# Two mixture-of-experts layers: more expert pairs ahead of the edge loop, exponentials at earlier places in it, and another order of the last combining

## The reference

```python
h = (x @ W_gat).reshape(M, 4, 4)                      # M rows, 4 heads, 4 experts
e = leaky_relu(a_src[src] + a_dst[dst])               # for each edge, and each token's own loop
alpha = softmax of e over the edges that share dst
agg = segment_sum(h[src] * alpha, dst)
scores = layernorm(agg + b_gat).mean over heads       # one number for each token and expert
w = softmax(top-2 of scores)                          # the gates
for ei in range(4):
    hh = gelu(x @ W1[ei] + b1[ei])                    # 256 -> 512
    out = out + gate[ei] * (hh @ W2[ei] + b2[ei])     # 512 -> 256
```

## Time and profile before

| | us |
|---|---|
| median of three runs | 4740.75 |
| profiled execution | 4737.15 |
| its span | 4735.4 |
| PE busy | 3592.8 (76%) |
| DVE busy | 3010.6 (64%) |
| ACT busy | 1489.1 (31%) |
| POOL busy | 1360.7 (29%) |

### The profile page before, as it was taken

How to read it: one execution, slowest core, us unless ns; L and a number is a source line. 1 busy time by engine, 2 the same in 40 slices (tenths; PEclk the granted TensorE clock), 3 DMA queues, 4 the chain that set the end, 5 groups by cost and what they waited for, 6 DMA issues and landing times. The chain is left out here.

```text
span 4735.4 us, 52627 instructions
## 1 busy us (share of the span) xinstructions
PE 3592.8 (76%) x17914; PEld 2038.7 (43%) x17914; DVE 3010.6 (64%) x6268; ACT 1489.1 (31%) x2073; POOL 1360.7 (29%) x1016
## 2 busy tenths in 40 slices
PE   5999999999589678862294984859868766157796
PEld 2333333333266346541162653646535544135464
DVE  3666666676588887889020277768988888602127
ACT  2556555555253012220041321225202121012221
POOL 2766667677300000007404101000000003723210
PEclk9999999999699888875697996869998887578898
DMA  3000000000351000001111183244100001111147
GB/s 126 10 28 28 19 10 28 27 28 19 114 179 53 8 19 32 31 28 13 19 63 28 62 326 131 76 173 143 42 5 36 23 27 26 13 25 57 36 156 281
DMA packets 144861, 301.63 MB, mean 64 GB/s; under 512 B 20580, under 2 KB 103140, under 8 KB 139492
## 3 DMA queue, kind: packets, MB, share of 16 engines
q1 hardware_dynamic: 98212, 180.78, 10.7%
q10 hardware_dynamic: 25920, 94.38, 5.2%
q0 software_dynamic: 20480, 23.14, 2.5%
HBM read 183.42 MB, written 114.81 MB: 63 GB/s over the span
## 5 line engine op out<-in xcount | busy, mean ns | idle before, releaser
L1083 PE MATMUL l_pu<-l_tt,l_w 128*128 128x512 f32 x2048 | 1034.2, 631 | 366.6 <-issue 187.8
L1094 PE MATMUL l_pd<-l_w,l_hid 128*128 128x256 f32 x4096 | 985.6, 385 | 164.8 <-ACT l_hid L1273 117.9
L1094 PEld LDWEIGHTS l_pd<-l_w,l_hid 128*128 128x128 f32 x4096 | 795.5, 194 | 501.3 <-issue 415.7
L1273 ACT ACTIVATE l_hid<-l_pu,l_b 128x512 f32<-128x512 f32 x512 | 349.7, 686 | 1661.6 <-PE l_pu L1083 1268.6
L389 DVE TENSOR_TENSOR at_pr<-at_ps,at_decay 128x1024 f32<-128x1024 f32 x512 | 601.1, 1217 | 182.2 <-PE at_ps L503 181.3
L1029 POOL DMA_INDIRECT l_g<-hs_rows,l_i_src x336 | 317.5, 945 | 1344.7 <-DVEq L1732 1236.7
L1083 PEld LDWEIGHTS l_pu<-l_tt,l_w 128*128 128x128 f32 x2048 | 407.1, 203 | 678.4 <-issue 655.9
L307 ACT ACTIVATE at_ab<-at_pr 128x1024 f32<-128x1024 f32 x512 | 537.2, 1055 | 439.7 <-DVE at_pr L389 392.5
L258 POOL TENSOR_TENSOR at_ab<-at_ab 128x1024 f32<-128x1024 f32 x256 | 600.8, 2370 | 178.2 <-ACT at_ab L307 178.2
L503 PE MATMUL at_ps<-at_qr,at_kr 32*128 32x512 f32 x2048 | 349.4, 644 | 14.8 <-issue 9.8
L1870 DVE SCALAR_TENSOR_TENSOR l_xo<-l_yb,l_gates,l_xo 128x256 f32<-128x256 f32 x448 | 187.3, 481 | 154.3 <-DMA l_yb<-ys 147.1
(11 more groups left out here) (341 smaller groups left out, 4191.1 us busy)
## 6 DMA issues: line engine op xcount, KB each, us to landing
ys<-l_yst ACTq DMA_DIRECT2D x112, 512.0 KB
l_yb<-ys SPq DMA_DIRECT2D x28, 2048.0 KB, 10.2
l_tt<-tT ACTq DMA_DIRECT2D x36, 512.0 KB, 3.3
at_xt<-in_x SPq DMA_DIRECT2D x16, 1024.0 KB, 5.4
l_xt<-x SPq DMA_DIRECT2D x32, 512.0 KB, 4.1
tT<-l_xnT ACTq DMA_DIRECT2D x32, 512.0 KB, 4.4
l_xo<-x SPq DMA_DIRECT2D x28, 512.0 KB, 4.6
x<-at_xt SPq DMA_DIRECT2D x8, 1024.0 KB, 4.3
```

The costliest lines, as they stand in the source:

```text
L1083: ins = pe.matmul(ps_u[q % 2][:, :], w1[:, e, c, P * q:P * q + P], tt[:, s, c, :], start=(c == 0), stop=(c == KK - 1))
L1094: ins = pe.matmul(out, hid[:, k % 2, c, P * r:P * r + P], w2[:, k % GE, c, :], start=False, stop=(c == MB - 1), skip_group_check=True)
L1273: act.activation(hid[:, k % 2, q, :], ps_u[q % 2][:, :], ACT.Gelu, bias=b1[:, k % GE, q:q + 1]).then_inc(s_act, 1)
```

## The change

The number of pairs ahead of the loop goes from 32 to 40, that in the loop from 24 to 16; direct pairs stay 8. The step counts follow: two more steps in the node blocks, 13 instead of 6 single steps in the first list, 14 instead of 10 in the late stage; what is left after the histogram goes from 14 steps to 33 (4 x 40 + 4 = 164 steps in all, of which 131 stand earlier). The exponentials stand after 24 and 40 of the loop's 68 steps, before after 41 and 66 of 100. The output buffers go from three to two. SP waits before its first loads of the tail only for the stores made ahead of the loop, and for the others before block 10. DVE and POOL take the ten stored blocks of the first pairs first, and the other four between the direct pairs. New lines shift the numbers after the change by 2 to 5.

```diff
-PRE_PAIRS = PAIRS // 2
+PRE_PAIRS = PAIRS // 2 + 8
-YB = 3
-PRE_NODES = (0, 0, 0, 1, 1, 1, 1, 1, 2, 2, 2, 2, 2, 2, 2, 2)
+YB = 2
+PRE_NODES = (0, 0, 0, 1, 1, 1, 2, 2, 2, 2, 2, 2, 2, 2, 2, 2)
-PRE_LATE = 10
+PRE_LATE = 14
-IN_SCAN = 41
-IN_MERGE = 66
+IN_SCAN = 24
+IN_MERGE = 40
...
-        TAIL_ORDER = [d for i in range(DIRECT) for d in [("stored", t) for t in range(i * STORED // DIRECT, (i + 1) * STORED // DIRECT)] + [("direct", i)]]
+        REST = STORED - BP
+        TAIL_ORDER = [("stored", t) for t in range(BP)] + [
+            d for i in range(DIRECT) for d in [("stored", BP + t) for t in range(i * REST // DIRECT, (i + 1) * REST // DIRECT)] + [("direct", i)]]
...
             for k in range(YB):
-                sp.wait_ge(s_y[k], n * (16 * LOOPED // YB) + 16 * ((PRE_PAIRS + YB - 1 - k) // YB))
-                sp.sem_inc(s_turn, 1)
+                sp.wait_ge(s_y[k], 16 * ((PRE_PAIRS + YB - 1 - k) // YB))
...
             for t in range(STORED):
                 b = t % 3
+                if t == BP:
+                    for k in range(YB):
+                        sp.wait_ge(s_y[k], n * (16 * LOOPED // YB) + 16 * ((PRE_PAIRS + YB - 1 - k) // YB))
+                        sp.sem_inc(s_turn, 1)
...
-                if h % (2 * IDX // RANK) == 2 * IDX // RANK - 1:
+                if h % (IDX // RANK) == IDX // RANK - 1:
                     pre(1)
...
-            pre(UNITS0 // 2)
+            pre(UNITS0)
```

## The result

The changed kernel takes 4703.18 us (median of 4 runs, 4700.86 to 4705.43), the kernel before on the same chip 4739.18 (4 runs, 4737.59 to 4741.27). The ratio is 0.9924, 95% interval 0.9907 to 0.9941: 36 us less, where 40 were forecast. The profiled execution took 4702.14, its span 4699.5.

The account below looks back on a forecast made before the run. The bound changes place: PE hangs on late ACT during gathers; DVE waits for exponentials and stored results. Per layer +85 - 86 - 20 = -21, for two -42: 4737.15 to 4695, median 3.6 above, 4699; range 4652 to 4744.

Parts of the forecast that it names:

- Ahead of the loop, +85: Work before the loop: 32 added steps per layer delay the start of POOL's gathers by 85 us.
- The last steps: After the histogram, 33 steps instead of 14: 19 uncovered steps at 3.44 us, +65.4 us per layer.
- The late steps: Late stage, 4 more steps: 13.8 us, inside PE's 18.27 us wait for DVE, so cost 0.
- nodes and list: Node blocks' two second steps, +2.7 us; first list's 7 more single steps at 2.4 us, +16.9 (bounds 0 and 29).
- In the loop, -86: Loop, per layer: earlier exponentials save 56 us at the first and 31 at the second, less 1 for the odd step.
- The odd shift of 17 steps: In the loop: ACT's late answer may fall on a step pair's other half, shifting the second exponential some 11 us either way.
- Gates, -1: When the gates are ready: +85 - 86 = -1 us, nearly where they were, at about 4521 in the old count.
- Tail, -20: Gates to end of span: 88 us for ten stored blocks plus 106 after, 194 against 213.8, so -20 per layer.
- The forecast of the ring: Tail buffers: combining 7.1, store 7.6, load 11.5, a round of 26.2 us; ten stored blocks take 88 us.
- Fast ring: Rival, 18%: tail loads keep up with DVE, ten blocks take 69 us instead of 88, 38 us less in all, 4661.
- Nothing left: Rival, 15%: single steps cost 29 us instead of 17, ten blocks 96 instead of 88; +20 a layer, 4737.
- Direct pairs at their old spacing: Rival, 12%: in the tail eight direct pairs take 138 us instead of 94; net +46 in all, 4787.

Follow-up runs that it names:

- new tail alone: Kernel before plus only SP's early loads and the new combining order, three buffers kept: 4692.8 us (0.9906) with late ACT, 4370.5 us (0.9895) with ACT in pace.

## Why the prediction was right, step by step

- **Ahead of the loop, +85.** Measured from the layer's start to the first gather: 923.2 - 840.4 = +82.8 in the first layer, +89.6 in the second. The last steps: +64.9 for 65.4. The late steps: covered. The rest, nodes and list, came to 18 and 25 us for 19.6; of it DVE's waits in the first list are 32.9 - 17.6 = 15.3 and 34.2 - 14.9 = 19.3, for 16.9.
- **In the loop, -86.** Measured 461.9 - 548.4 = -86.5 in the first layer and -86.0 in the second. The two waits are 55.2 and 22.1, where 57 and 20 were forecast. The odd shift of 17 steps did not move ACT's late answers by a noticeable amount.
- **Gates, -1.** Counted from each layer's own start (1276.3 and 3117.8, before 1275.9 and 3137.9) they moved by -3.7 us in the first layer and +3.6 in the second. The new tail alone, with none of the first two parts, has its gates at 4500.4, and the changed kernel on that same chip has them at 4500.9. This is the direct proof that the two large terms cancel there.
- **Tail, -20.** Ten blocks 87 us for 88, PE stood 26.45 for 26, gates to end 4699.5 - 4504.67 = 194.8 for 194; before 214.2, so -19.4. In the first layer, from its gates to the start of the second, 473.2 went to 456.4: -16.8. So the layers gained 20.5 and 15.8 us where 21 each were forecast, and most of the 6 us missing is in the +89.6 and the -16.8. The forecast of the ring, a round of 26.2 us for three buffers, held against the rival in which the ring keeps up with DVE (69 us). DMA engines were at 0.93 there: the loads are what DVE waited for. Some luck is in these hits. The first buffer's three rounds took 20.9, 33.5 and 25.8 us, 26.7 in the mean. A load took 13.1 us and a store 5.1 in the median, where 11.5 and 7.6 were put in, and only their sum was right. After the ten blocks the prediction's terms (2.3, 89.5, 4, 1.0 and 8.1) add up to 105 and not to the 106 it wrote; 107.2 were measured, and the single stored blocks, taken at 4 us, cost PE nothing once it ran.
- **The fit that it quoted.** By the fit of the Trainium skill, page "DMA: Bandwidth & Descriptors", section "Anatomy of one DMA — SWDGE (gpsimd) path", the ring would have kept up with DVE. That fit is for transfers that POOL issues; the 2 MB loads here are issued by SP, with others in flight, and took 13.1 us, not 6.8. The stretch from 4520 to 4605 moved 357 GB/s, where DVE's own pace would have needed 456. The prediction was right to go by its rows.
- **Its range.** The ends, 4652 and 4744, don't follow from the terms that they name: half the single steps' cost is 8.5 us a layer, so 4644, and 11 us a layer on top of 4737 give 4759. The measured 4703 lies well inside either.
- **The rivals.** Fast ring: out, by the seven waits for stored results and 87 us. Nothing left: out, a single step in the list cost 2.4 us and not 4.1, and the ring did not go at 10.4 us a block. Direct pairs at their old spacing: out, eight took 98.7 us (94 were forecast), not 138, because PE sets them: between stored blocks DVE takes one instruction of a pair each 6.89 us and waits 6.01 of it for PE.
- **What it had wrong without harm.** It counted the new order into the tail's gain. The old order with early loads does as well (190.2): with the new one DVE's blocks delay the first direct pair, with the old one PE's arrival does. And it spoke of the late ACT as a property of the stage. It holds on some chips only, and the forecast of -86 in the loop hangs on it: on a chip in pace the exponentials gave nothing back, and moved as early in the kernel before they cost 116 us. The rows of one chip could not show this; the forecast held because the changed kernel was measured on the same chip as the rows.

## What to carry to other kernels

Before moving work ahead of a point to fill waits, ask who reaches that point last. Here 19 steps that nothing covered, with 18 to 25 us of smaller costs, pushed the critical gathers back by as much as the earlier exponentials recovered, and the free gain was a load that had been waiting for stores it didn't need. When several edits come together, price each against the kernel without the others: one of three, alone, gave as much as all three. A place in a queue that is tuned on one chip can be wrong on the next when an engine's pace differs: a wait whose releaser is another engine's data (ACT for l_xm) is a sign that the place is already early.

## What the hardware showed

- **ACT's pace beside indirect gathers differs from chip to chip.** With 168 gathers issued 1.25 us apart, one kernel took 386.9 us from the first gather to the gates on one chip and 548.0 on another. Chips 6 and 14 were late, as the first one was, 3 and 5 in pace, and on each the kernel before kept to one pace (4729 to 4746 us or 4410 to 4422). None of these four was measured on two occasions, so a cause in the occasion is not excluded. How late: in the new tail alone PE finished the hidden rows' product at 2165.0, and ACT's gelu of it started at 2194.05, 29 us later; PE went on 1.1 us after that. Where it is late, ACT's answers stand in a pattern, here in the new tail alone, first layer:

```profile
2160.45 0.69 ACT L1278 ACTIVATE l_hid<-l_pu,l_b 128x512 f32<-128x512 f32 x1 [9.74 <-remote]
2194.05 0.69 ACT L1278 ACTIVATE l_hid<-l_pu,l_b 128x512 f32<-128x512 f32 x1 [32.91 <-issue]
2216.45 0.60 ACT L1292 ACTIVATE l_yst<-l_pd 128x512 f32<-128x512 f32 x1 [21.71 <-issue]
...
2227.66 0.69 ACT L1278 ACTIVATE l_hid<-l_pu,l_b 128x512 f32<-128x512 f32 x1 [9.45 <-issue]
```

The starts are 33.6, 22.4 and 11.2 us apart, multiples of 11.2, the time of 9 gathers. The lateness ends some 22 us after the last gather is issued (in the changed kernel 4255.4, and ACT's last late answer at 4277.19). The waits name no engine. Register-valued waits on ACT were ruled out above; what the cause is stays open.

- **The granted clock followed PE's work.** In the same 110 us it was 1.00 where PE was busy throughout and 0.59 where it was busy 22.74 us: the higher of its two levels, 2.4 GHz, throughout in the one, and mostly the lower, 1.2 GHz, in the other.
